# Four chained graph layers on one core: hand-written orders for the first three iterations, more load semaphores, and the 512-to-256 product summed in two halves

## The chip, the core and the metric

One Trainium2 chip, one of its cores, float32 inputs and outputs. The metric is the device time in microseconds (us) of one launch, from the first to the last instruction and what lies around them. TensorE is PE, VectorE is DVE, ScalarE is ACT, GpSimd is POOL, SyncE (which issues every transfer) is SP.

## What is computed

128 graphs of 128 nodes with 256 features, and an adjacency matrix per graph, pass four residual layers, each ended by a normalization over the features:

```python
x = _layernorm(x + _L0_gnn_ref(x, adj, W1, b1, gamma, beta, W2, b2), axis=-1)   # hypergraph convolutions 256->512->256
x = _layernorm(x + _L1_gnn_ref(x, adj, W), axis=-1)                             # x and its mean over neighbours, 512->256
x = _layernorm(x + _L2_gnn_ref(x, adj, W1, b1, W2, b2, W3, b3), axis=-1)        # three graph convolutions
x = _layernorm(x + _L3_gnn_ref(x, adj, kernel), axis=-1)                        # one more, masked where x is all zero
```

## The kernel before

Two graphs make a pair, and there are 64 pairs. The work on a pair is cut into stages, and a software pipeline runs them: in iteration n the first layer's stages work on pair n and n-1, the second's on n-2, the third's on n-3 and n-4, the fourth's on n-4 and n-5 (the table `LAG`). Iterations 0 to 7 and the last ones are unrolled, those between run in a hardware loop of four iterations a turn (`steps`, L175). Each engine runs one function `body(n, k)`, in which the order of its stages is written by hand; a stage that has no pair yet is skipped. Engines are tied by semaphores alone, and each engine's instructions run in the written order, so a wait holds everything behind it on that engine.

Products in high precision are split: a float32 matrix is rounded to `_hi`, the rest is `_lo`, and `product` (L257) issues three matmuls for each block: hi by hi, hi by lo, lo by hi. ACT makes most `_hi`, DVE or POOL the `_lo`.

The stages on PE that the prediction speaks of, for a pair p: `G` (operands BH, HT), its transpose `Tr` (ident, Gd), `Gx` (GT, x_in), `R` (24 matmuls of 256 columns, w1T by gx, the 256-to-512 product), `P` (L367: 24 matmuls of 258 columns, r by w2c, the 512-to-256 product, and two of one column, sq by ones, for the mean square), `GP` (p_f, GT), `xT` (ident, x), `XAB` (x1T by wab), `AXB` (xbw by A), `Ax2` (A_f, x), then `H1` and the others of the later layers. PSUM has eight banks of 512 columns; `BANK` gives each stage its own, and P uses two, one per graph.

P before: for each graph 12 matmuls over all four blocks of r and then its one-column matmul. It waits at its start for `r_hi[1]`, `r_lo` and `sq_sum`:

```python
pe.wait_ge(r_hi[1], upto(p))
pe.wait_ge(r_lo, upto(p))
pe.wait_ge(sq_sum, upto(p))
```

POOL makes r_lo in two halves (L978, L980) with one semaphore after the second, then adds the squares (L983, L985), then A_lo.

In the first iterations there is also the work on the weights, which are loaded into buffers that later hold data: w1T is split into hi (ACT, L466) and lo (POOL, L957); w2 is scaled (`scale_w2`, L686 and L688), its column means come from four matmuls with ones (w2g, ones), it is centred and split (`centre_w2`, L694 to L708), and beta by w2 is four matmuls (n_s, beta_b); wab, the three v and wk are split as well, the last four on POOL in iteration 1. DVE's edge counts of a pair (`prep`: L791 HT to L825 be_parts) and the scaling of G (L786, L795, L801, L811 Gd) are mixed in one sequence. DVE begins with constants and then waits for three small loads that share the semaphore `small_loaded`.

## Time and profile before

| | us |
|---|---|
| median of 3 runs | 1478.44 (1476.14 to 1479.6) |
| the profiled execution | 1476.8 |
| its span, first to last instruction | 1475.0 |
| PE busy | 1419.1 (96%) |
| DVE busy | 1152.0 (78%) |
| ACT busy | 1050.5 (71%) |
| POOL busy | 887.7 (60%) |

Matmuls are pipelined and overlap, so PE's busy time is time in which at least one is under way. The clock column of the windows gives the share of TensorE's full clock that was granted. A timeline merges equal instructions that follow each other: start, length, engine, line, operation, and in brackets the engine's idle time before it and what ended it.

### The profile page before, as it was taken

Reading aid. Unit: us, or ns where it says so; the run is one execution under the profiler, and the core shown is the slowest. Engines: PE = TensorE matmul, PEld = TensorE weight load, DVE = VectorE, ACT = ScalarE, POOL = GpSimd, SP = SyncE. Lnnn points to the kernel's source line nnn. Section 1 sums busy time; section 2 is a strip of 40 time slices with the busy share of each in tenths; the row PEclk is TensorE's granted clock in tenths of the full one; section 3 lists DMA queues with packets and bytes.
Section 4 is the critical chain, followed back from the end, with each engine's and each line's share of the span. In section 5 each row is a group of like instructions: output and inputs, shape, how many; then the busy total and the mean of one; then the engine's idle time right before and its main releaser. Section 6 shows DMA issues by size and latency. Waiting matters only on the chain. (4 is left out here: it accounts for less than half of the span.)

```text
span 1475.0 us, 34371 instructions
## 1 busy us (share of the span) xinstructions
PE 1419.1 (96%) x10896; PEld 1352.9 (92%) x10896; DVE 1152.0 (78%) x4063; ACT 1050.5 (71%) x2377; POOL 887.7 (60%) x841
## 2 busy tenths in 40 slices
PE   4899999999999999999999999999999999999974
PEld 4799999999999999999999999999999999999974
DVE  5678887887887878878878878788788788787763
ACT  3477777777777777777777777777777777767753
POOL 4455765665665665675675576566566566566542
PEclk9999999999999999999999999999999999999997
DMA  3001011011001001101101101101101100110000
GB/s 123 22 23 37 19 38 36 18 36 36 23 31 36 25 29 36 35 19 36 36 18 36 36 18 36 36 18 36 36 18 36 36 25 28 36 33 12 16 15 22
DMA packets 29419, 45.45 MB, mean 31 GB/s; under 512 B 3392, under 2 KB 11712, under 8 KB 29376
## 3 DMA queue, kind: packets, MB, share of 16 engines
q1 hardware_dynamic: 29376, 44.91, 9.5%
q8 instruction: 22, 0.36, 0.1%
q14 instruction: 21, 0.17, 0.0%
HBM read 28.12 MB, written 16.78 MB: 30 GB/s over the span
## 5 line engine op out<-in xcount | busy, mean ns | idle before, releaser
L957 POOL TENSOR_TENSOR h_lo<-h_f,h_hi 128x512 fp32r<-128x512 f32 x128 | 164.6, 1286 | 338.9 <-ACT h_hi L466 338.9
L714 DVE BATCH_NORM_STATS2 n_st<-n_s 128x6 f32<-128x256 f32 x512 | 188.6, 411 | 7.5 <-POOL n_s L990 5.2
L481 ACT ACTIVATE n_std<-n_mv,eps_c 128x2 f32<-128x2 f32 x256 | 74.7, 292 | 166.7 <-DVE n_mv L719 166.5
L972 POOL TENSOR_TENSOR n_s<-tk,mask 128x512 f32<-128x512 f32 x64 | 66.6, 1040 | 168.6 <-issue 82.8
L255 PE MATMUL psum<-w2c_hi,r_hi 128*128 128x258 f32 x512 | 150.4, 294 | 6.4 <-POOL sq L985 4.7
L255 PE MATMUL psum<-v_hi,h_hi 128*128 128x256 f32 x512 | 149.8, 292 | 5.0 <-issue 5.0
L494 ACT ACTIVATE h_f<-psum,columns 128x256 f32<-128x256 f32 x256 | 107.5, 471 | 54.4 <-PE psum L255 54.4
L255 PE MATMUL psum<-w2c_lo,r_hi 128*128 128x258 f32 x512 | 145.5, 284 | 0.0
L255 PE MATMUL psum<-v_lo,h_hi 128*128 128x256 f32 x512 | 145.4, 284 | 0.0
L255 PE MATMUL psum<-v_hi,h_lo 128*128 128x256 f32 x512 | 145.1, 283 | 0.0
L255 PE MATMUL psum<-gx_hi,w1T_hi 128*128 128x256 f32 x512 | 143.3, 280 | 1.3 <-DVE gx_lo L663 1.3
L255 PE MATMUL psum<-w2c_hi,r_lo 128*128 128x258 f32 x512 | 144.4, 282 | 0.0
L255 PE MATMUL psum<-gx_hi,w1T_lo 128*128 128x256 f32 x512 | 142.9, 279 | 0.0
L255 PE MATMUL psum<-gx_lo,w1T_hi 128*128 128x256 f32 x512 | 142.9, 279 | 0.0
L255 PE MATMUL psum<-A_f,x 128*128 128x128 f32 x1024 | 137.3, 278 | 4.8 <-ACT x L588 3.9
L255 PEld LDWEIGHTS psum<-A_f,x 128*128 128x128 f32 x1024 | 127.0, 194 | 5.2 <-ACT x L588 4.2
L978 POOL TENSOR_TENSOR r_lo<-r_f,r_hi 128x512 fp32r<-128x512 f32 x64 | 83.2, 1301 | 58.4 <-ACT r_hi L466 58.3
L255 PE MATMUL psum<-wab_hi,x1T_hi 128*128 128x512 f32 x256 | 106.8, 417 | 1.5 <-ACT x1T_hi L466 1.5
L663 DVE TENSOR_TENSOR ax_lo<-psum,ax_hi 128x512 fp32r<-128x512 f32 x128 | 87.9, 687 | 25.8 <-ACT ax_hi L466 25.8
L588 ACT ACTIVATE x<-n_s,n_shift,n_rstd 128x256 f32<-128x256 f32 x128 | 70.1, 595 | 48.6 <-DVE n_shift L731 48.6
L255 PEld LDWEIGHTS psum<-w2c_hi,r_hi 128*128 128x128 f32 x512 | 97.6, 191 | 7.1 <-issue 7.1
L255 PEld LDWEIGHTS psum<-v_hi,h_hi 128*128 128x128 f32 x512 | 97.8, 191 | 5.5 <-issue 5.5
(154 smaller groups left out, 5344.2 us busy)
## 6 DMA issues: line engine op xcount, KB each, us to landing
x_in<-x_in_dram SPq DMA_DIRECT2D x64, 256.0 KB, 2.6
out<-x SPq DMA_DIRECT2D x64, 256.0 KB, 2.0
at_in<-adjT SPq DMA_DIRECT2D x64, 128.0 KB, 2.1
r_f<-w1T_in SPq DMA_DIRECT2D x1, 512.0 KB, 5.4
n_s<-w2T_in SPq DMA_DIRECT2D x2, 256.0 KB, 5.7
h_f<-wab_in SPq DMA_DIRECT2D x2, 256.0 KB, 6.1
rows<-rows_in SPq DMA_DIRECT2D x1, 256.0 KB, 4.5
xa<-v_in SPq DMA_DIRECT2D x1, 256.0 KB, 6.0
```

Source lines behind the costliest of these rows:

```text
L255: return pe.matmul(o, a, b, start=start, stop=stop)
L481: act.activation(nm.std[:], nm.mv[:, :, 1], ACT.Sqrt, bias=eps_c[:, 0:1]).then_inc(nm.rooted, 1)
L494: return act.activation(dst[:, m].rearrange("p g c -> p (g c)"), psum[:, BANK[stage] + extra, (m % 2) * 2 * C:(m % 2 + 1) * 2 * C], ACT.Re ...
L588: last = act.activation(x3[:, g, :], n3.s[:, g, :], ACT.Identity, scale=n3.rstd[:, g:g + 1], bias=n3.shift[:, g:g + 1])
L663: return dve.tensor_tensor(dst[1][:], src, f(dst[0][:]), ALU.subtract).then_inc(signal, 1)
L714: last = dve.bn_stats(nm.st[:, g, :], nm.s[:, g, :])
L957: return pool.tensor_tensor(dst[1][:], src, f(dst[0][:]), ALU.subtract).then_inc(signal, 1)
L972: pool.tensor_tensor(n4.s[:], tk[:], bc(mask[:], [C, 2, D], 2), ALU.mult).then_inc(tk_masked, 1)
L978: pool.tensor_tensor(r_s[1][:, 0:2], r_f[:, 0:2], f(r_s[0][:, 0:2]), ALU.subtract)
```

## The change

The first three iterations (n = 0, 1, 2; `FILL = 3`) no longer come from `body` but from a function `fill` on each engine with its own order. The stages have become small functions that both `fill` and `body` call; for n of 3 and more the written order is as before. In the fill three stages use other banks (`bank`). The loads have more semaphores and another order, w1T is loaded and split in two halves, and its lo part is made on DVE instead of POOL. The three v and wk are loaded into buffers that are free until later (x3, x4, tk), so their splits can stand at the end of the fill. `P` sums the first two blocks of r for both graphs and then the other two, and `r_lo` has a semaphore for each half. Cut to its core:

```diff
+        def bank(stage, pair):
+            filling = isinstance(pair, int)
+            if filling and stage == "Tr" and pair in (1, 2):
+                return 3
+            if filling and stage == "GP" and pair == 0:
+                return 2
+            if filling and stage == "xT" and pair == 0:
+                return 6
+            return BANK[stage]
...
-            load(0, 0)
-            sp.dma_start(ident[:], eye).then_inc(small_loaded, 16)
-            sp.dma_start(columns_s[:], columns).then_inc(small_loaded, 16)
-            sp.dma_start(rows_b[:], rows.partition_broadcast(C)).then_inc(small_loaded, 16)
...
+            def fill():
+                sp.dma_start(at_in[:, 0], adjT[0]).then_inc(at_loaded[0], 16)
+                sp.dma_start(ident[:], eye).then_inc(eye_loaded, 16)
+                sp.dma_start(columns_s[:], columns).then_inc(columns_loaded, 16)
+                sp.dma_start(x_in[:, 0], x[0]).then_inc(x_loaded[0], 16)
+                for h in range(2):
+                    sp.dma_start(w2T_f[h], w2T[:, 2 * h:2 * h + 2]).then_inc(w2_loaded, 16)
+                for h in range(2):
+                    half = slice(h * 2 * C, (h + 1) * 2 * C)
+                    sp.dma_start(w1T_f[:, :, half], w1T[:, :, half]).then_inc(w1_loaded[h], 16)
+                load(1)
+                sp.dma_start(rows_b[:], rows.partition_broadcast(C)).then_inc(rows_loaded, 16)
+                for kk in range(KD):
+                    sp.dma_start(wab_f[kk], wab[:, kk]).then_inc(wab_loaded, 16)
+                load(2)
+                for dst, src in ((v_f[0], v1), (v_f[1], v2), (v_f[2], v3), (wk_f, wk)):
+                    sp.dma_start(dst, src).then_inc(v_loaded, 16)
+                load(3)
+                input_free(0)
+                load(4)
 
             def body(n, k):
-                if first(n, 0):
...
+            def P(n, k):
+                p = n - 1
+                if first(n, 1):
+                    pe.wait_ge(w2c_lo, 1)
+                if begun(n - 2):
+                    if not first(n, 2):
+                        pe.wait_ge(x1T_lo, upto(n - 2))
+                    pe.wait_ge(p_made, upto(n - 2))
+                for h in range(2):
+                    pe.wait_ge(r_lo[h], upto(p))
+                    for g in range(2):
+                        product(psum[:, BANK["P"] + g, 0:D + 2],
+                                [(part(r_s, ALL, m, g), part(w2c_s, ALL, m)) for m in (2 * h, 2 * h + 1)],
+                                start=h == 0, stop=h == 1)
+                pe.wait_ge(sq_sum, upto(p))
+                for g in range(2):
+                    last = mm(psum[:, BANK["P"] + g, D + 2:D + 3], sq1[:, g, :], ones[:, 0:1], True, True)
+                last.then_inc(pe_did["P"], 1)
...
+            def fill():
+                G(0, 0)
+                Tr(0, 0)
+                Gx(0, 0)
+                w2_columns()
+                R(1, 1)
+                G(1, 1)
+                Tr(1, 1)
+                Gx(1, 1)
+                P(1, 1)
+                betaW_rows()
+                R(2, 2)
+                GP(1, 1)
+                G(2, 2)
+                P(2, 2)
+                xT(2, 2)
+                Tr(2, 2)
+                Gx(2, 2)
+                XAB(2, 2)
+                GP(2, 2)
+                AXB(2, 2)
             def body(n, k):
                 if active("R", n):
...
+            def fill():
+                act.wait_ge(consts_step, 1)
+                act.activation(h_std[:, 0:1], eps_c[:], ACT.Sqrt).then_inc(table_loaded, 1)
+                act.wait_ge(table_loaded, 1)
+                act.wait_ge(columns_loaded, 16)
+                copy_GT(0, 0)
+                split_w1(0)
+                split_gx(0, 0)
+                split_w1(1)
+                relu_r(1, 1, 0)
+                round_r(1, 1, 0)
+                relu_r(1, 1, 1)
+                round_r(1, 1, 1)
+                square_r(1, 1)
+                copy_GT(1, 1)
+                split_gx(1, 1)
+                copy_A(1, 1)
+                act.wait_ge(wab_loaded, 16 * KD)
+                for kk in range(KD):
+                    copy(wab_s[0][:, kk], wab_f[kk]).then_inc(wab_hi, 1)
+                square_mean(1, 1)
+                root_h(1, 1)
+                relu_r(2, 2, 0)
+                round_r(2, 2, 0)
+                relu_r(2, 2, 1)
+                round_r(2, 2, 1)
+                root(n1, 0)
+                square_r(2, 2)
+                copy_A(2, 2)
+                split_x1T(2, 2)
+                square_mean(2, 2)
+                copy_GT(2, 2)
+                root_h(2, 2)
+                split_gx(2, 2)
+                act.wait_ge(v_loaded, 16 * 4)
+                for dst, src in ((v_s[0], v_f[0]), (v_s[1], v_f[1])):
+                    copy(dst[0][:], src).then_inc(v_hi, 1)
+                out_XAB(2, 2)
+                for dst, src in ((v_s[2], v_f[2]), (wk_s, wk_f)):
+                    copy(dst[0][:], src).then_inc(v_hi, 1)
+                root(n1, 1)
+                root(n2, 0)
             def body(n, k):
...
+                prep(-1, -1)
+                scale_G(0, 0)
+                dve.wait_ge(columns_loaded, 16)
+                dve.wait_ge(w2_loaded, 16 * 2)
+                for m in range(KH):
+                    dve.tensor_scalar(w2g[:, m, :], w2T_f[m // 2][:, m % 2], gamma_c[:, m:m + 1], None,
+                                      ALU.mult).then_inc(w2_scaled, 1)
+                split_w1(0)
+                split_gx(0, 0)
+                split_w1(1)
+                dve.wait_ge(w2_sums, 1)
+                dve.tensor_scalar(w2mean[:], psum[:, 2, 0:D], 1.0 / DH, None, ALU.mult).then_inc(w2_mean, 1)
+                prep(0, 0)
+                dve.wait_ge(w2_mean, 1)
+                dve.wait_ge(w2_scaled, KH)
+                dve.tensor_tensor(w2g[:], w2g[:], bc(w2mean[:], [C, KH, D], 1), ALU.subtract).then_inc(w2_centred, 1)
+                dve.wait_ge(w2_centred, 1)
+                dve.tensor_copy(w2c_s[0][:, :, 0:D], w2g[:]).then_inc(w2c_hi, 1)
+                scale_G(1, 1)
+                dve.wait_ge(w2c_hi, 1)
+                dve.tensor_tensor(w2c_s[1][:, :, 0:D], w2g[:], f(w2c_s[0][:, :, 0:D]),
+                                  ALU.subtract).then_inc(w2c_lo, 1)
+                split_gx(1, 1)
+                for m in range(KH):
+                    dve.tensor_scalar(beta_b[:, m, :], ones[:], beta_c[:, m:m + 1], None,
+                                      ALU.mult).then_inc(beta_made, 1)
+                dve.wait_ge(rows_loaded, 16)
+                dve.tensor_scalar(b2half[:], rows_b[:, 0], 0.5, None, ALU.mult).then_inc(consts_made, 1)
+                prep(1, 1)
+                dve.wait_ge(betaW_sums, 1)
+                dve.tensor_copy(betaW[:], psum[:, 3, 0:D]).then_inc(betaW_made, 1)
+                wide_var(1, 1)
+                wide_invert(1, 1)
+                make_p(1, 1)
+                dve.wait_ge(wab_hi, KD)
+                for kk in range(KD):
+                    dve.tensor_tensor(wab_s[1][:, kk], wab_f[kk], f(wab_s[0][:, kk]),
+                                      ALU.subtract).then_inc(wab_lo, 1)
+                sum_n1(1, 1)
+                stats_alone(n1, 0)
+                make_x1(2, 2)
+                scale_G(2, 2)
+                split_x1T(2, 2)
+                wide_var(2, 2)
+                wide_invert(2, 2)
+                make_p(2, 2)
+                split_gx(2, 2)
+                prep(2, 2)
+                split_xbw(2, 2)
+                sum_n1(2, 2)
+                stats_alone(n1, 1)
+                node_degree_max(2, 2)
+                node_degree_recip(2, 2)
+                make_agg(2, 2)
+                sum_n2(2, 2)
+                stats_alone(n2, 0)
+                invert(n2, 0)
+                shift(n2, 0)
...
+            def low_r(n, k, h):
+                p = n - 1
+                pool.wait_ge(r_hi[h], upto(p))
+                if begun(p - 1):
+                    pool.wait_ge(pe_did["P"], upto(p - 1))
+                half = slice(2 * h, 2 * h + 2)
+                pool.tensor_tensor(r_s[1][:, half], r_f[:, half], f(r_s[0][:, half]),
+                                   ALU.subtract).then_inc(r_lo[h], 1)
...
+            def fill():
+                make_BH(-1, -1)
+                make_BH(0, 0)
+                low_r(1, 1, 0)
+                low_r(1, 1, 1)
+                add_squares(1, 1)
+                low_A(1, 1)
+                make_BH(1, 1)
+                make_xb(1, 1)
+                low_r(2, 2, 0)
+                low_r(2, 2, 1)
+                add_squares(2, 2)
+                low_A(2, 2)
+                make_xb(2, 2)
+                make_BH(2, 2)
+                pool.wait_ge(v_hi, 4)
+                for dst, src in ((v_s[0], v_f[0]), (v_s[1], v_f[1]), (v_s[2], v_f[2]), (wk_s, wk_f)):
+                    lo(dst, src, v_lo)
 
             def body(n, k):
-                if first(n, 0):
-                    pool.wait_ge(w1_loaded, 16)
-                    pool.wait_ge(w1_hi, 1)
```

Where the instructions now stand. TensorE, from the end of the first R to the second R; gx and w1T are R's operands, n_s and beta_b those of beta by w2, w2c and r those of P. Before:

```order
L255 MATMUL psum<-gx_hi,w1T_lo 128x256
L255 MATMUL psum<-n_s,beta_b 128x256 x4
L255 MATMUL psum<-BH,HT 128x130 x4
L255 MATMUL psum<-w2c_hi,r_hi 128x258
...
L255 MATMUL psum<-ones,sq 128x1
...
L255 MATMUL psum<-ones,sq 128x1
L402 MATMUL psum<-ident,Gd 128x128 x2
L255 MATMUL psum<-GT,x_in 128x128 x4
L255 MATMUL psum<-p_f,GT 128x256 x2
L255 MATMUL psum<-gx_hi,w1T_hi 128x256
```

Now:

```order
L279 MATMUL psum<-gx_hi,w1T_lo 128x256
L279 MATMUL psum<-BH,HT 128x130 x4
L329 MATMUL psum<-ident,Gd 128x128 x2
L279 MATMUL psum<-GT,x_in 128x128 x4
L279 MATMUL psum<-w2c_hi,r_hi 128x258
...
L279 MATMUL psum<-w2c_hi,r_lo 128x258
L279 MATMUL psum<-ones,sq 128x1 x2
L279 MATMUL psum<-n_s,beta_b 128x256 x4
L279 MATMUL psum<-gx_hi,w1T_hi 128x256
...
L279 MATMUL psum<-p_f,GT 128x256 x2
```

Tr and Gx of pair 1 have moved ahead of P of pair 0, beta by w2 behind it, and R of pair 1 ahead of GP; the rows left out repeat the three operand pairs of the product.

VectorE, from its constants to the first split of gx. Before:

```order
L678 TENSOR_SCALAR w2c_lo<-ones 128x4 x2
L680 TENSOR_SCALAR b2half<-rows 128x256
L791 TENSOR_SCALAR HT<-at_in 128x256
L798 TENSOR_REDUCE ht_count<-HT 128x2
...
L825 TENSOR_TENSOR be_parts<-be_parts,be_r 128x2
L786 TENSOR_SCALAR dn_max<-psum 128x2
L791 TENSOR_SCALAR HT<-at_in 128x256
L795 RECIPROCAL dn_inv<-dn_max 128x2
L798 TENSOR_REDUCE ht_count<-HT 128x2
L801 SCALAR_TENSOR_TENSOR dinv<-psum,dn_inv 128x2
...
L811 TENSOR_TENSOR Gd<-psum,dinv 128x256
```

Now:

```order
L1024 TENSOR_SCALAR w2c_lo<-ones 128x4 x2
L903 TENSOR_SCALAR HT<-at_in 128x256
L907 TENSOR_REDUCE ht_count<-HT 128x2
...
L928 TENSOR_TENSOR be_parts<-be_parts,be_r 128x2
L881 TENSOR_SCALAR dn_max<-psum 128x2
L885 RECIPROCAL dn_inv<-dn_max 128x2
L889 SCALAR_TENSOR_TENSOR dinv<-psum,dn_inv 128x2
L896 TENSOR_TENSOR Gd<-psum,dinv 128x256
L1031 TENSOR_SCALAR w2g<-n_s,columns 128x256 x4
L1008 TENSOR_TENSOR w1T_lo<-r_f,w1T_hi 128x2x256
L817 TENSOR_TENSOR gx_lo<-psum,gx_hi 128x512
```

The edge counts of pair 0 (HT to be_parts) no longer stand behind b2half, the scaling of G of pair 0 (dn_max to Gd) no longer has the edge counts of pair 1 mixed into it, and half of w1T's lo part has come from POOL.

ScalarE, from the relu of pair 1 (r_f) to A, in iteration 2. Before:

```order
L481 ACTIVATE n_std<-n_mv,eps_c 128x2
L494 ACTIVATE r_f<-psum,columns 128x256 x4
L466 ACTIVATE x1T_hi<-psum 128x512
L466 ACTIVATE r_hi<-r_f 128x512 x2
L547 ACTIVATE sq<-r_f 128x1024
L466 ACTIVATE A_hi<-at_in 128x256
L466 ACTIVATE A_f<-at_in 128x256
```

Now:

```order
L591 ACTIVATE r_f<-psum,columns 128x256 x2
L567 ACTIVATE r_hi<-r_f 128x512
L591 ACTIVATE r_f<-psum,columns 128x256 x2
L567 ACTIVATE r_hi<-r_f 128x512
L581 ACTIVATE n_std<-n_mv,eps_c 128x2
L622 ACTIVATE sq<-r_f 128x1024
L567 ACTIVATE A_hi<-at_in 128x256
L567 ACTIVATE A_f<-at_in 128x256
L567 ACTIVATE x1T_hi<-psum 128x512
```

The square of r (sq) now stands behind n_std of pair 0, and x1T_hi behind A.

## Rows read from the trace of the kernel before

**Rows 1.** Windows: us, then PE, PEld, DVE, ACT, POOL busy, clock, DMA share, GB/s.

```profile
0.00:62.26 62.26, 37.03 (x225) 32.69 (x225) 36.26 (x120) 22.78 (x50) 25.57 (x29) 0.97 0.26 86
...
96.20:1388.40 1292.20, 1290.69 (x10032) 1234.76 (x10031) 1047.05 (x3710) 959.27 (x2181) 809.90 (x765) 1.00 0.09 29
...
1388.40:1475.00 86.60, 58.49 (x399) 54.47 (x397) 44.10 (x161) 46.21 (x98) 30.55 (x26) 0.86 0.05 19
```

**Rows 2.** Timeline of PE in the fill: start, us, engine, line, operation [idle before].

```profile
10.37 1.12 PE L255 MATMUL psum<-BH,HT 128*128 128x130 f32 x4 [10.37 <-POOL BH L1001]
...
13.91 0.66 PE L402 MATMUL psum<-ident,Gd 128*128 128x128 f32 x2 [2.42 <-DVE Gd L811]
...
15.05 2.08 PE L255 MATMUL psum<-GT,x_in 128*128 128x128 f32 x8 [0.47 <-ACT GT L466]
...
20.12 0.47 PE L255 MATMUL psum<-gx_hi,w1T_hi 128*128 128x256 f32 x1
...
23.06 1.89 PE L255 MATMUL psum<-n_s,beta_b 128*128 128x256 f32 x8
...
30.06 0.36 PE L255 MATMUL psum<-w2c_hi,r_hi 128*128 128x258 f32 x1 [4.72 <-POOL sq L985]
...
38.77 0.47 PE L255 MATMUL psum<-gx_hi,w1T_hi 128*128 128x256 f32 x1
```

**Rows 3.** Windows, the same columns: the start of P of pair 0.

```profile
30.00:34.00 4.00, 3.94 (x20) 3.97 (x21) 0.00 (x0) 0.00 (x0) 4.00 (x5) 0.57 0.00 0
```

**Rows 4.** Timeline of DVE in the fill.

```profile
7.16 0.29 DVE L680 TENSOR_SCALAR b2half<-rows 128x256 f32<-128x256 f32 x1 [5.30 <-DMA rows<-rows_in]
...
7.37 0.29 DVE L791 TENSOR_SCALAR HT<-at_in 128x256 fp32r<-128x256 f32 x1
...
8.83 0.15 DVE L825 TENSOR_TENSOR be_parts<-be_parts,be_r 128x2 f32<-128x2 f32 x1
...
11.62 1.16 DVE L791 TENSOR_SCALAR HT<-at_in 128x256 fp32r<-128x256 f32 x1
...
13.35 0.42 DVE L811 TENSOR_TENSOR Gd<-psum,dinv 128x256 f32<-128x256 f32 x1
...
39.88 0.75 DVE L714 BATCH_NORM_STATS2 n_st<-n_s 128x6 f32<-128x256 f32 x2
...
48.90 0.68 DVE L847 TENSOR_TENSOR xbw_lo<-psum,xbw_hi 128x512 fp32r<-128x512 f32 x1
```

**Rows 5.** The tile at_in up to 40 us: how long its five loads took.

```profile
DMA to landing us min/median/max: 2.1/6.0/6.9
```

**Rows 6.** Timeline of POOL in the fill.

```profile
9.14 1.18 POOL L1001 TENSOR_TENSOR BH<-HT,be_parts 128x256 fp32r<-128x256 f32 x2 [8.68 <-DVE be_parts L825]
...
27.75 1.27 POOL L983 TENSOR_TENSOR sq<-sq 128x512 f32<-128x512 f32 x1
...
29.09 0.72 POOL L985 TENSOR_TENSOR sq<-sq 128x256 f32<-128x256 f32 x1
```

**Rows 7.** Timeline of ACT, iterations 2 and 3.

```profile
44.60 1.05 ACT L547 ACTIVATE sq<-r_f 128x1024 f32<-128x1024 f32 x1
...
59.59 1.07 ACT L514 ACTIVATE x<-n_s,n_shift,n_rstd 128x256 f32<-128x256 f32 x2
...
60.57 1.54 ACT L494 ACTIVATE r_f<-psum,columns 128x256 f32<-128x256 f32 x4
```

**Rows 8.** Timeline of PE in the loop: between the graphs of P.

```profile
703.27 0.28 PE L255 MATMUL psum<-ones,sq 128*128 128x1 f32 x2
703.41 0.37 PE L255 MATMUL psum<-w2c_hi,r_hi 128*128 128x258 f32 x1
703.62 0.28 PE L255 MATMUL psum<-w2c_lo,r_hi 128*128 128x258 f32 x1
```

**Rows 9.** Waits of the weight loads, 140 to 1400 us: total, times, longest.

```profile
PEld psum L255 <- DVE p_f L895: 9.7, 45, 0.3
```

**Rows 10.** Timeline of ACT in the loop.

```profile
706.87 0.15 ACT L597 ACTIVATE h_mean<-psum 128x2 f32<-128x2 f32 x1
```

More of the change, by code:

```diff
@@ L27 @@
 BANKS = 8
+FILL = 3
 UNROLL = 4
@@ new lines, in betaW_rows @@
+            def betaW_rows():
+                pe.wait_ge(beta_made, KH)
+                for m in range(KH):
+                    last = mm(psum[:, 3, 0:D], beta_b[:, m, :], w2T_f[m // 2][:, m % 2], m == 0, m == KH - 1)
+                last.then_inc(betaW_sums, 1)
+            def fill():
[19 more added lines that the diff above has]
+                AXB(2, 2)
```

953 lines of the change are left out of this document (499 added, 454 removed).

## The prediction

> **What bounds it now.** I read the windows first, then the timeline of each engine in the fill, then the loop. They cut the span at 62.26 us, the start of the first Ax2, where the full pipeline begins, and where the drain begins. Between, PE is busy 1290.69 of 1292.20 us; before the first Ax2 it is busy 37.03 of 62.26, after the loop 58.49 of 86.60 [rows 1]. So of PE's idle time 25.2 us lie in the fill, 1.5 in the middle and 28.1 in the drain. The change rewrites the fill and leaves the drain's order. Since the middle has no slack on PE, an Ax2 that comes earlier ought to move the end by as much.
>
> The timeline of PE in the fill shows where the 25.2 us are: 10.37 before the first G, released by POOL's BH; 2.42 before Tr, released by DVE's Gd; 4.72 before P of pair 0, released by POOL's sum of squares; the rest in pieces of 1.6 us or less [rows 2]. It shows a second loss too. P of pair 0 starts after that idle stretch, and from 30 to 34 us the granted clock is 0.57, so mostly the lower of the two levels, 1.2 GHz instead of 2.4 [rows 3].
>
> **The start.** DVE does nothing for 5.30 us but wait for the third of three loads under one semaphore, though the edge counts behind it need only at_in [rows 4]. Now they wait for that alone. It is still the first load, issued at 0.75, and the quickest at_in landed 2.1 us after its issue [rows 5], at 2.9. The counts take 1.6 (7.37 to the end at 8.98), POOL's BH 1.35 with its start delay (8.98 to 10.32) [rows 4, 6]. G starts at about 5.9: **4.5 us less idle**.
>
> G takes 1.12 us. The scaling of G took 2.24 us to the end of Gd at 13.77, as it was mixed with the next pair's counts, HT's 1.16 among them [rows 4]. Alone it is three small steps at 0.2 (as between the small steps before be_parts) and Gd's 0.42, so Tr waits 1.2, not 2.42: **1.2 less**. GT and Gx follow at their old distances. From Gx to R it was 5.07 us (15.05 to 20.12) [rows 2]; in it the work on w2 hides gx's split and now hides w1T's lo, whose two halves cost DVE 1.3 in place of one long one on POOL. R of pair 0 comes at 14.5 instead of 20.1.
>
> **From R to the second iteration.** Before, P waited 4.72 us for relu, rounding, r_lo and squares. Now G, Tr and Gx of pair 1 stand there, and P asks for the squares (1.27 and 0.72 on POOL [rows 6]) at its end only. The new order has its own waits. R ends at 17.4; w2mean, the counts (1.6) and BH (1.35) let G start at 17.9: 0.5. Tr waits for DVE: 1.1. Gx waits for the copy of GT: 0.5. P then finds r_lo made, and the lower clock should not come, as no idle stretch here is longer than 1.2 us where the one before P was 4.72. The window has 20 matmuls in 4.0 us; at the 0.12 of R (24 in 2.94 us) they take 2.4: **1.6 us of busy time less** [rows 2, 3].
>
> So Tr stands at 19.6, Gx at 20.6, P at 21.6. P is 26 matmuls, 3.1 us, beta by w2 1.5 (23.06 to the next work at 24.6), and R of pair 1 comes near 26.2, not 38.77 [rows 2]; with its 2.94, GP's 1.0 and G's half of 1.12 P of pair 1 starts near 30.7 and its product ends at 33.6, but its squares come late: on ACT the root of n1 now stands ahead of the square, and that root waits for GP, the sum, and the statistics (0.75 and 0.3) on DVE, until about 32.2; then 1.05 on ACT and 2.1 on POOL [rows 4, 6, 7]. PE waits **1.8**. Behind it stand xT, Tr, Gx and all that follows. Then 0.95 before Gx of pair 2 (x1T_hi and h_mean lie ahead of GT on ACT); 1.0 before AXB (xbw_hi and xa, each about half of sq's 1.05, and xbw_lo's 0.68 on DVE, less GP's length [rows 4, 7]).
>
> **Into iteration 3.** From AXB's end DVE has two small steps (0.4), agg and the sum of n2 (0.7 to 0.9 each, as xbw_lo), the statistics (1.05), then with ACT's root three small steps (0.9), and only then x1 for xT (0.75): 4.9 to 5.2 with the delays. R and G cover 3.5; with what n1's own statistics push DVE back, xT waits 1.9. ACT's x (1.07) and four relus (1.54) [rows 7] stand before Ax2: 1.3 more.
>
> **The sum of the fill.** Idle after: 5.9 + 1.2 + 0.5 + 0.5 + 1.1 + 0.5 + 1.8 + 0.95 + 1.0 + 1.9 + 1.3 = 16.65 us, against 25.2: 8.6 less. With the clock's 1.6 that is **10.2 us**, Ax2 at 52 instead of 62.26. Two prices the trace doesn't show. When the clock rises: before, the matmuls ran slow until about 20.1, after 5 us of nearly unbroken work; now such work begins at 9.4. If it rises as late against that, R runs at full rate; if R runs at the lower level throughout, it takes 24 x 0.1 = 2.4 us more. I take 0.3, for the full case is the nearest row. And POOL's four splits of v and wk (512 columns and some 1.3 each, as the first sum of squares [rows 6]), which lay under P, now lie over DVE's chain into iteration 3. HT took 0.29 us with POOL idle, but 1.16 where POOL worked [rows 4]; the price is from nothing to twice that 0.87. I take 0.5. The fill gives 10.2 - 0.8 = 9.4, with bounds 7 to 11.
>
> The Trainium skill (SBUF — State Buffer, "Who interferes with whom") says that a VectorE operation with two SBUF inputs and a GpSimd operation that reads SBUF exclude each other for the whole instruction. By it the sum and x1 of that chain could each wait out a full split, 2.6 us in all by the row above.
>
> **P in two halves, in the loop.** Nothing waits there for r_lo. But the one-column matmuls are now together at the end. Before, the first stood between the graphs: it starts at 703.27, graph 1's first product at 703.41, its second at 703.62, so 0.21 us for a step that elsewhere takes 0.12 [rows 8]. Over 64 pairs the 0.085 saved would be 5.4 us. I don't count on it. In 45 of the 58 iterations between 140 and 1400 us the weight load of GP waited for p_f [rows 9]. p_f hangs on h_mean. ACT began it at 706.87 with no idle time before it [rows 10], while P's last matmul, twelve steps of 0.12 behind 703.41, had started at 704.9. So ACT's own queue sets that moment, not P, and what P saves the wait for p_f takes. At the 13 others up to 0.085 each may stay: 0 to 5.4 us, I take **0.6**, near the lower end, for most iterations wait.
>
> The drain keeps its order; its stretches at the lower clock may fall otherwise, 1 us either way, taken as nothing.
>
> **Sum.** 9.4 + 0.6 = 10.0 us off. The profiled execution took 1476.8, which is 1.6 below the median of the runs shown, well within their spread. From it the result is 1466.8; against the median of 1478.44 it is **1468.4 us**, which I forecast, 0.7% faster. About 0.2%, 3 us, is what a measurement of this kernel tells from no change.
>
> **Rivals.**
>
> *Half of it* (0.15). The new waits are longer than reckoned: the square behind n1's root, the collision with POOL, w2 landing late, R at the lower clock. Each alone costs 1 to 2.5 us; two or three together leave 4 to 6: 1473.4. For it: every stage I moved is on a chain of four engines with little cover. Against: the first wait's 4.5 us depends on one load only.
>
> *The loop keeps P's saving* (0.12). If the ring gets shorter with P, 5.4 instead of 0.6: 1463.6. For it: in 13 iterations PE didn't wait. Against: the 45.
>
> *Alternating banks cost time* (0.03). Now P goes graph 0, 1, 0, 1, two more changes of bank a pair, 128 in all, and leaves an accumulation open in each. The middle has no slack, so it pays all of it: from 10.0/128 = 0.08 us a change the gain is gone. If a change had to let the matmul before it end, 0.28 instead of 0.12 [rows 8], it costs 0.16, 20.5 us in all: 1488.9, slower. Against: PE is busy without a break through the middle although XAB changes banks as well [rows 1].
>
> The Trainium skill (TensorE: Matmul & The Clock Gate, "A second HAM failure mode: psum-queue depth-cycling") warns of just that: a kernel that cycled through PSUM banks kept falling to the lower clock between its matmul groups. With P at 1.2 GHz in every iteration 24 x 0.1 x 64 would be 150 us more. The clock column reads 1.00 through the loop [rows 1], and by the rule it should not.
>
> *It does not do what it says* (0.03). Something in the middle sets the end by itself, or what starts early waits in iterations 3 to 7: 1478. Against: PE's 1.5 us of idle in the middle.
>
> The forecast has 0.67. Faster by over 0.2% holds it, the half and the loop's saving, 0.94; within 0.2% 0.03; slower 0.03. The range takes the bounds of the fill and of the loop (11 + 5.4 off: 1462.0) and reaches over the half: 1462.0 to 1474.0.
>
> **What would show it.** PE's first G at 5.9, not 10.4; R of pair 0 at 14.5; no clock below full between 14.5 and the drain; the wait for sq before P's last matmuls in iteration 2, near 1.8; the first Ax2 at 52 to 53; the loop's period as it was, with more wait for p_f. Wrong if Ax2 is early and the end is not, or if the iterations' period changed by more than 0.1 us.

## The result, and the profile after

The changed kernel took **1472.1 us**, the median of 6 runs (1469.8 to 1472.7). Before took 1478.1 us beside it, in 6 runs. The ratio is 0.9957, with a 95% interval from 0.9944 to 0.9969: 6.0 us faster, where 10.0 was forecast. The profiled execution took 1472.7 us with a span of 1470.8, that is 4.1 and 4.2 us less than the profiled one of before. So the traces show 4.2 of the 6.0 us.

| | before | after |
|---|---|---|
| median, us | 1478.1 | 1472.1 |
| span of the profiled run | 1475.0 | 1470.8 |
| first G | 10.37 | 5.86 |
| R of pair 0 | 20.12 | 14.32 |
| R of pair 1 | 38.77 | 29.57 |
| first Ax2 | 62.26 | 56.10 |
| GP of iteration 3 | 74.7 | 69.4 |
| last GP | 1410.0 | 1405.0 |
| from there to the end | 65.0 | 65.8 |

So in the profiled executions the fill gave 6.2 us up to the first Ax2 and 5.3 up to GP of iteration 3, the loop kept all but 0.3 of that, and the drain lost 0.8.

The timeline of PE in the fill answers to [rows 2]. These are its waits, each with its releaser, and two of the operations that ran slowly:

```profile
5.86 1.12 PE L279 MATMUL psum<-BH,HT 128*128 128x130 f32 x4 [5.86 <-POOL BH L1233]
8.17 0.66 PE L329 MATMUL psum<-ident,Gd 128*128 128x128 f32 x2 [1.20 <-DVE Gd L896]
9.39 2.08 PE L279 MATMUL psum<-GT,x_in 128*128 128x128 f32 x8 [0.56 <-ACT GT L567]
...
19.55 0.66 PE L279 MATMUL psum<-BH,HT 128*128 128x130 f32 x4 [1.70 <-POOL BH L1233]
...
21.31 0.44 PE L329 MATMUL psum<-ident,Gd 128*128 128x128 f32 x2 [1.10 <-DVE Gd L896]
22.22 2.08 PE L279 MATMUL psum<-GT,x_in 128*128 128x128 f32 x8 [0.47 <-ACT GT L567]
...
27.95 1.97 PE L279 MATMUL psum<-n_s,beta_b 128*128 128x256 f32 x8
29.57 0.47 PE L279 MATMUL psum<-gx_hi,w1T_hi 128*128 128x256 f32 x1
...
34.90 0.36 PE L279 MATMUL psum<-w2c_hi,r_hi 128*128 128x258 f32 x1 [0.89 <-POOL r_lo L1213]
...
54.36 0.66 PE L394 MATMUL psum<-ident,x 128*128 128x128 f32 x4 [3.26 <-DVE x L857]
56.10 1.95 PE L279 MATMUL psum<-A_f,x 128*128 128x128 f32 x8 [1.08 <-ACT r_f L591]
```

The first three waits are as forecast (5.9, 1.2, 0.5). The fourth, before G of pair 1, is 1.70 where 0.5 was forecast, and xT of iteration 3 waits 3.26, not 1.9. The same Gx takes 1.16 us at full clock (at 41.04) and 2.08 at 22.22; Ax2 took 1.13 before and takes 1.95.

The windows say why (us, then PE, PEld, DVE, ACT, POOL busy, clock, DMA share, GB/s). They answer to [rows 3]:

```profile
18.00:22.00 4.00, 1.10 (x6) 0.72 (x6) 2.64 (x7) 2.55 (x6) 4.00 (x5) 1.00 0.00 0
22.00:25.00 3.00, 2.78 (x13) 2.78 (x14) 1.06 (x2) 0.83 (x3) 2.89 (x2) 0.51 0.00 0
...
51.00:56.00 5.00, 0.76 (x5) 0.42 (x4) 2.73 (x11) 2.88 (x8) 1.71 (x2) 1.00 0.01 2
56.00:59.00 3.00, 2.90 (x11) 2.74 (x12) 0.97 (x2) 2.39 (x5) 1.96 (x2) 0.53 0.00 0
```

From 18 to 22 us PE was busy 1.10 of 4.00 us, six matmuls with no gap above 1.7 us around them; then the granted clock is the lower level, 1.2 GHz, for about 3 us of nearly unbroken work. From 51 to 56 it was busy 0.76 of 5.00, with one gap of 3.26 us, and the same follows. The slow stretch of before is gone, and two others have come. (The clock column can't be read at the very start: up to 14 us it says 1.00, though the first Gx takes 2.08 us, as it does later at 0.51.)

Two collisions of DVE and POOL stand behind the two long waits. POOL's timeline first, then DVE's:

```profile
16.95 2.55 POOL L1233 TENSOR_TENSOR BH<-HT,be_parts 128x256 fp32r<-128x256 f32 x2 [11.14 <-DVE be_parts L928]
```

```profile
16.78 1.22 DVE L1041 TENSOR_TENSOR w2g<-w2g,w2mean 128x1024 f32<-128x1024 f32 x1
...
49.84 1.74 DVE L993 SCALAR_TENSOR_TENSOR n_s<-agg,x 128x512 f32<-128x512 f32 x1
```

BH takes 1.18 when DVE leaves it alone [rows 6], and 2.55 beside the centring of w2 and the rounding behind it. The sum of n2 takes 0.68 in the loop and 1.74 here, beside POOL's splits of v.

In the loop, the waits of the weight loads (total, times, longest) answer to [rows 9], and GP of iterations 3 and later, first and last start, shows the loop's length, of before and of after:

```profile
PEld psum L279 <- DVE p_f L964: 11.1, 55, 0.3
```

```profile
L255 PE MATMUL psum<-p_f,GT x248: 379/379/483, 74.7 to 1410.0; 128*128 128x256 f32 x124
```

```profile
L279 PE MATMUL psum<-p_f,GT x248: 379/379/483, 69.4 to 1405.0; 128*128 128x256 f32 x124
```

That is 62 groups of four matmuls, so 61 intervals, and the 0.8 us from the first to the last matmul of the last group: together 1335.3 us before, 1335.6 after, 21.9 us an iteration in both. So P's saving in the loop is nothing. Below, "the 61 intervals" are counted in this same way.

### The profile page after: what moved, and what is told of

The parts are those of the page before. It is cut to its first block and busy times, and to the rows that moved or that the text cites. A ratio compares the mean times of both kernels' runs of the same rounds, so it can differ in the third digit from the quotient of the medians.

```text
span 1470.8 us, 34536 instructions
## 1 busy us (share of the span) xinstructions
PE 1420.3 (97%) x10896; PEld 1355.6 (92%) x10896; DVE 1151.5 (78%) x4066; ACT 1051.4 (71%) x2378; POOL 889.0 (60%) x840
## 5 line engine op out<-in xcount | busy, mean ns | idle before, releaser
L586 ACT ACTIVATE x<-n_s,n_shift,n_rstd 128x256 f32<-128x256 f32 x384 | 208.6, 591 | 65.9 <-DVE n_shift L847 63.1
L1213 POOL TENSOR_TENSOR r_lo<-r_f,r_hi 128x512 fp32r<-128x512 f32 x128 | 164.0, 1304 | 38.2 <-ACT r_hi L567 38.1
L279 PE MATMUL psum<-w2c_hi,r_hi 128*128 128x258 f32 x512 | 145.0, 283 | 0.9 <-POOL r_lo L1213 0.9
L591 ACT ACTIVATE r_f<-psum,columns 128x256 f32<-128x256 f32 x256 | 99.1, 463 | 4.1 <-PE psum L279 4.1
```

What stands on the lines that cost most here:

```text
L279: return pe.matmul(o, a, b, start=start, stop=stop)
L586: last = act.activation(dst[:, g, :], nm.s[:, g, :], ACT.Identity, scale=nm.rstd[:, g:g + 1], bias=nm.shift[:, g:g + 1])
L591: return act.activation(dst[:, m].rearrange("p g c -> p (g c)"), psum[:, BANK[stage] + extra, (m % 2) * 2 * C:(m % 2 + 1) * 2 * C], ACT.Re ...
L1213: pool.tensor_tensor(r_s[1][:, half], r_f[:, half], f(r_s[0][:, half]), ALU.subtract).then_inc(r_lo[h], 1)
```

## The experiments

The runs of before beside these had medians of 1477.7 us (b_start, b_p, a_old_p, a_veps), 1477.4 (b_order, a_prep, a_sq, a_v), 1477.1 (a_alt, a_warm, a_nov) and 1477.8 (a_best). Each ratio is to these. After was not run again beside them, only before: what is said "under after" or "above after" sets medians of different sets of runs side by side and is good to about 1 us.

### The start alone, in the kernel before

b_start moves two waits, and the step on b2half that hangs on one of them, and nothing else:

```diff
-            dve.wait_ge(small_loaded, 16 * 3)
-            dve.tensor_scalar(b2half[:], rows_b[:, 0], ...)
+                if first(n, 0):          # behind prep of pairs 0 and 1
+                    dve.wait_ge(small_loaded, 16 * 3)
+                    dve.tensor_scalar(b2half[:], rows_b[:, 0], ...)
                     scale_w2()
-            pool.wait_ge(consts_made, 1)  # from POOL's start to ahead of w1T's low part
```

> The kernel before, with one thing of the change: DVE's wait for the three small loads and POOL's wait for b2half move behind the edge counts of pairs 0 and 1. My theory: this alone gives the start's 4.5 us. First G at 5.9, R of pair 0 at 15.6 instead of 20.1, time 1478.1 - 4.5 = 1473.6. Rival: the loads of w1T and w2T, which keep their place behind the rows, bound R and the centring of w2; then R moves by 2 us or less and the time is 1476 or more.

1476.5 us, ratio 0.9993 (0.9984 to 1.0002): no difference that can be measured. Its timeline of PE has the early G, and behind it a new wait:

```profile
5.88 1.11 PE L255 MATMUL psum<-BH,HT 128*128 128x130 f32 x4 [5.88 <-POOL BH L999]
12.51 0.66 PE L402 MATMUL psum<-ident,Gd 128*128 128x128 f32 x2 [5.52 <-DVE Gd L808]
```

DVE's timeline names what stood in front:

```profile
11.08 0.29 DVE L788 TENSOR_SCALAR HT<-at_in 128x256 fp32r<-128x256 f32 x1 [3.89 <-DMA at_in<-adjT]
```

In DVE's queue of before, the counts of pair 1 are interleaved with the scaling of G of pair 0, and they wait for at_in of pair 1, which comes behind w1T and w2T. My theory fell, and so did the rival, which named R and w2. The semaphore only pays with the order.

b_order adds that order (scaling of G, scaling of w2, then the counts of pair 1):

```diff
+                if first(n, 0):
+                    ...  # degree_max, recip, inverse and Gd of pair 0
+                    dve.wait_ge(small_loaded, 16 * 3)
+                    ...
+                    scale_w2()
+                    ...  # HT, ht_count, be, be_parts of pair 1
+                else:
+                    ...  # interleaved as before
```

> The kernel before with its own wait for at_in as in b_start, and DVE's order of the first iteration changed too: the scaling of G of pair 0 and of w2 first, then the edge counts of pair 1. In b_start the first G came at 5.9 but Tr then waited 5.5 us, since in DVE's queue the counts of pair 1 stood between the steps of the scaling and waited for at_in of pair 1. My theory: it takes both, the semaphore and the order. Tr at 8.2, Gx at 9.4, R of pair 0 between 14.5 and 17 (w1T and w2T set it), and the time 2 to 4.5 us under before: 1473.2 to 1475.7. Rival: P of pair 0 hangs on the chain from w2's load through w2's centring, and nothing is gained: 1477.

1473.8 us, ratio 0.9979 (0.9970 to 0.9989). Tr came at 8.21, but R of pair 0 only at 17.8. DVE waited 2.25 us for w2T, which lies behind w1T in SP's queue, and then its first scaling of w2 took 2.44 us instead of the 0.34 of the next ones:

```profile
10.52 2.44 DVE L683 TENSOR_SCALAR w2g<-n_s,columns 128x256 f32<-128x256 f32 x1 [2.25 <-DMA n_s<-w2T_in]
```

Beside it POOL split w1T from 10.47 to 12.82, the work that the change gives to DVE. The gain is 3.6 us, inside the expectation. The profiled execution doesn't show it: it was the slowest of the 11 (1477.2), R of pair 0 came early, but the clock was at the lower level in parts of 25 to 40 us, and the first Ax2 stood at 63.27, behind the 62.26 of before. So the semaphore and DVE's order together are shown to pay; that the rest of the change's start comes from SP's order and from w1T's split on DVE is read off these waits and not tested alone.

### P in two halves

b_p is the kernel before with P, and the two semaphores of r_lo, as in the change's diff. a_old_p is the changed kernel with the old P from iteration 3 on, and a_alt changes graph with every matmul there:

```diff
 a_old_p
-                    for h in range(2):
-                        pe.wait_ge(r_lo[h], upto(p))
-                        for g in range(2):
-                            product(..., start=h == 0, stop=h == 1)
-                    pe.wait_ge(sq_sum, upto(p))
+                    for h in range(2):
+                        pe.wait_ge(r_lo[h], upto(p))
+                    pe.wait_ge(sq_sum, upto(p))
+                    for g in range(2):
+                        product(...)
+                        last = mm(psum[:, BANK["P"] + g, D + 2:D + 3], sq1[:, g, :], ones[:, 0:1], True, True)
 a_alt
-                    for h in range(2):
-                        for g in range(2):
-                            product(psum[:, BANK["P"] + g, 0:D + 2], [... for m in (2 * h, 2 * h + 1)])
+                    for m in range(KH):
+                        for x, y in ((0, 0), (0, 1), (1, 0)):
+                            for g in range(2):
+                                mm(psum[:, BANK["P"] + g, 0:D + 2], r_s[x][:, m, g], w2c_s[y][:, m], ...)
```

> The kernel before, with the two-half P alone, in the fill and the loop. My theory: in the fill P of pair 0 no longer waits for the two sums of squares, 1.27 + 0.72 us, and the loop keeps nothing: 1478.1 - 2.0 = 1476.1, with a period of 21.8 to 22.2 us per four... that is, per iteration group as before and more wait for p_f than 9.7 us. Rival, the loop keeps 0.085 us a pair: 1476.1 - 5.4 = 1470.7. Rival, alternating banks cost 0.16 us a change: above 1490.

1475.6 us, ratio 0.9984 (0.9975 to 0.9993): 2.1 us less, as expected. P of pair 0 waited 1.18 for r_lo, not 4.72 for the squares, and started at 28.06 instead of 30.06, though the first G came 1.2 us later. The 61 intervals took 1335.8 us. This profiled execution too was the slowest of its 11 (1478.3): from 40 to 47 us its clock was at the lower level, and what P had gained was gone at the first Ax2 (63.58).

> The changed kernel, but from iteration 3 on P goes graph by graph as before, each with its one-column matmul behind it. My theory: the loop's saving was all taken by the wait for p_f, so the time stays within 0.6 us of 1472.1 and the wait for p_f falls from 11.1 to about 9.7 us. Rival, the loop kept part of it: up to 1477.5. Rival, the changes of bank cost something: below 1471.

1473.3 us, ratio 0.9965 (0.9952 to 0.9979). GP of iteration 3 and the last one started at 69.4 and 1404.8, so the 61 intervals took 1335.4 us against 1335.6: the loop's length doesn't depend on the form of P. The median is 1.2 above after, outside the expected 0.6, but the two intervals overlap, and the trace has the same loop and the same start of GP. The expected size of the wait was wrong as well: it is 11.6 us, not 9.7. The listed total of that wait is no ledger for the time.

> The changed kernel, from iteration 3 on P changes graph, and so PSUM bank, with every matmul: 23 changes a pair in place of 3, with the same matmuls. My theory: a change of bank costs nothing; time within 0.7 of after, matmuls of P 0.12 us apart. Rival: a change costs 0.01 us or more: 20 x 61 x 0.01 = 12 us and above, 1484.

1474.5 us, ratio 0.9981 (0.9971 to 0.9990). That is 2.4 above after and outside the expected 0.7, but not in the loop. There the 61 intervals took 1335.6 us, as in after. The matmuls of P, now merged in pairs over the two graphs, begin 0.24 us apart, 0.12 each, and the clock of the window is full:

```profile
701.15 0.40 PE L279 MATMUL psum<-w2c_hi,r_hi 128*128 128x258 f32 x2
701.39 0.41 PE L279 MATMUL psum<-w2c_lo,r_hi 128*128 128x258 f32 x2
701.63 0.40 PE L279 MATMUL psum<-w2c_hi,r_lo 128*128 128x258 f32 x2
```

```profile
66.00:1385.00 1319.00, 1316.93 (x10233) 1261.73 (x10232) 1066.42 (x3759) 975.54 (x2217) 826.91 (x782) 1.00 0.09 29
```

A change of bank costs nothing here. The 4.5 us by which GP of iteration 3 comes later in its profiled run (73.9) lie in the fill, whose orders are those of after: Gx of pair 2, and XAB behind it, ran at the lower clock there, Gx in 2.08 us where after had 1.16. Which short stretches of the fill fall to the lower level differs between runs of one and the same order.

### Three reorderings in the fill

```diff
 a_prep (DVE)
+                prep(0, 0)
                 dve.wait_ge(w2_sums, 1)
                 dve.tensor_scalar(w2mean[:], psum[:, 2, 0:D], ...)
-                prep(0, 0)
 a_sq (ACT)
-                root(n1, 0)
                 square_r(2, 2)
+                root(n1, 0)
 a_v (ACT, then POOL)
                 square_mean(1, 1)
+                act.wait_ge(v_loaded, 16 * 4)
+                for dst, src in (...): copy(dst[0][:], src).then_inc(v_hi, 1)   # from around out_XAB(2, 2)
                 root_h(1, 1)
...
-                make_BH(2, 2)
                 pool.wait_ge(v_hi, 4)
                 for dst, src in (...): lo(dst, src, v_lo)
+                make_BH(2, 2)
```

> The changed kernel with DVE's edge counts of pair 1 ahead of w2mean, in the 1.5 us in which DVE waited for w2's sums. My theory: the missed 1.2 us before G of pair 1 come from POOL's BH (2.55 us beside DVE's centring of w2, 1.19 alone). BH starts at 15 and ends before R does; G of pair 1 waits 0 to 0.2 us instead of 1.7, Gx of pair 1 starts at 20.6, and if the clock does not fall before it, it takes 1.16 instead of 2.08 us. Time 1.5 to 3 us under after: 1469 to 1470.5. Rival: the collision only moves, since w2's centring now meets BH earlier or r_lo; P of pair 0 waits for w2c_lo instead, and the time stays within 0.7 of after.

> The changed kernel with ACT's square of pair 1 ahead of the root of n1. My theory: the wait before P's last matmuls in iteration 2 (0.90 us) goes, and xT of pair 0, already late, does not come later as DVE waits 0.3 us at most. First Ax2 0.8 us earlier, time 0.8 under after: 1471.3. Rival: Gx of pair 2 and xT wait longer by what was gained (x1 later): no change.

> The changed kernel with the splits of v and wk earlier: ACT's four high parts while it waits before root_h of pair 0, POOL's four low parts between xb and BH of iteration 2, where POOL was idle for 4.4 us and DVE's long operations read PSUM. My theory: the sum of n2 took 1.74 us beside POOL's splits; it takes 0.69 now, xT of iteration 3 waits 2.2 instead of 3.26 us, the first Ax2 comes 1.0 us earlier, and with less idle time the clock may hold, which gives 1 us more. Time 1 to 2.5 us under after: 1469.6 to 1471. Rival: BH of pair 3, now behind the splits, makes G late by what is gained, or the clock falls in any case: within 0.5 of after.

Their medians are 1470.6 (ratio 0.9942 to 0.9969), 1471.0 (0.9941 to 0.9968) and 1471.4 us (0.9945 to 0.9973), the second as expected, the first and third 0.1 and 0.4 above the ranges. The intervals overlap that of after, so the times alone don't prove a gain; the traces show each wait. In a_prep the wait before G of pair 1 is gone, and the first Ax2 comes at 54.05 instead of 56.10. BH still took 2.17 us beside the centring, but it began 2.0 us earlier. In a_sq the wait for the squares is 0.37 instead of 0.90, not gone, and the first Ax2 comes at 55.22. In a_v the sum of n2 took 0.69, and xT waits 2.20:

```profile
53.30 0.69 DVE L991 SCALAR_TENSOR_TENSOR n_s<-agg,x 128x512 f32<-128x512 f32 x1
```

```profile
56.78 0.66 PE L394 MATMUL psum<-ident,x 128*128 128x128 f32 x4 [2.20 <-DVE x L855]
```

In its profiled run that gain was lost (the first Ax2 at 58.51), as Gx of pair 2 and XAB behind it fell to the lower clock:

```profile
41.00:48.00 7.00, 6.30 (x19) 0.51 0.17 56
```

In this row the columns are us, PE busy, clock, DMA share and GB/s.

### The clock

a_warm puts matmuls whose results nobody uses ahead of PE's waits, 29 in the fill and 60 in the drain (not 64, as the expectation says):

```diff
+            WARM = {(1, 'G'): 5, (1, 'Tr'): 4, (1, 'Gx'): 1, (2, 'AXB'): 4, (3, 'xT'): 12, (3, 'Ax2'): 3,
+                    (65, 'xT'): 8, (65, 'AXB'): 8, ...}
+            def warm(n, stage):
+                for _ in range(WARM.get((n, stage), 0) if isinstance(n, int) else 0):
+                    mm(psum[:, 6 if n < 4 else 5, 0:2 * D], w1T_s[0][:, 0, 0:C], w1T_s[0][:, 0, 0:2 * D], True, True)
             def G(n, k):
+                warm(n, "G")
```

> The changed kernel with idle work for PE: matmuls of 512 columns into an unused bank stand ahead of waits, 5, 4 and 1 of them before G, Tr and Gx of pair 1, 4 before AXB of iteration 2, 12 and 3 before xT and Ax2 of iteration 3, and 64 in the drain before its longer waits, each group some 20% shorter than the wait. Nothing else changes, their results are not used. My theory: the clock fell to the lower level twice in the fill (22 to 25.5 and 56 to 59 us) because PE had been mostly idle in the 4 us before each, and that is the missing part of the forecast. With this work the clock stays at the upper level; the first P starts 0.9 us earlier, the first Ax2 takes 1.13 instead of 1.95 us and the fill gives 2.5 to 3.5 us; the drain, where 10 of 60 us run at the lower level, gives 1 to 3 us more. Time 3.5 to 6 us under after: 1466 to 1468.6. Rival: the clock falls on its own schedule whatever PE does, and the added matmuls delay the real ones: 1472 or more.

1463.7 us, ratio 0.9912 (0.9897 to 0.9927): **8.4 us under after** by the medians, 7.4 if each is taken against the before beside it, and more than expected. The clock stays up in both stretches. The windows of a_warm, with the columns of the first windows above:

```profile
18.00:22.00 4.00, 3.34 (x20) 2.52 (x21) 2.70 (x5) 1.27 (x2) 4.00 (x4) 1.00 0.00 0
22.00:25.00 3.00, 3.00 (x29) 3.00 (x27) 2.21 (x6) 2.25 (x5) 2.37 (x3) 1.00 0.03 8
...
51.00:56.00 5.00, 4.07 (x22) 3.08 (x22) 2.00 (x6) 5.00 (x11) 1.73 (x2) 1.00 0.00 2
56.00:59.00 3.00, 3.00 (x21) 2.70 (x20) 3.00 (x10) 1.84 (x5) 2.92 (x4) 1.00 0.00 0
```

The drain, of after and then of a_warm (us, PE busy, clock, DMA share, GB/s):

```profile
1400.00:1436.00 36.00, 27.35 (x184) 0.91 0.04 15
```

```profile
1400.00:1436.00 36.00, 32.50 (x217) 1.00 0.04 15
```

GP of iteration 3 came at 65.4 instead of 69.4, which is 4.0 us from the fill, the 61 intervals took 0.6 less, and from the last GP to the end it took 61.2 instead of 65.8 us, 4.6 from the drain. Of the 4.0 not all is the idle matmuls' work, for R of pair 0 already began 1.05 us earlier, and the first idle matmul stands behind it. R's first matmul in after, and then in a_warm:

```profile
14.32 0.78 PE L279 MATMUL psum<-gx_hi,w1T_hi 128*128 128x256 f32 x1
```

```profile
13.27 0.47 PE L279 MATMUL psum<-gx_hi,w1T_hi 128*128 128x256 f32 x1
```

Up to there both have the same order; what differs is when the matmuls on w2 pass from the slow pace to the fast one (in a_veps R began at 13.31, in a_nov at 13.48). That leaves about 3.0 us in the fill for the idle matmuls, an estimate from one execution of each. The Trainium skill (TensorE: Matmul & The Clock Gate, "The HAM clock gate") says that the gate follows how busy PE has been lately; the rows agree, with the clock at 0.51 behind 1.10 us of work in 4.00 and at 1.00 behind 3.34. The runs of a_warm lie within 1.2 us (4 runs), those of after within 2.9.

### What the wait for p_f costs

```diff
 a_veps
-                dve.scalar_tensor_tensor(out=h_veps[:], in0=h_var[:], scalar=LN_EPS,
-                                         in1=eps_c[:].to_broadcast([C, 2]), op0=ALU.add, op1=ALU.max)
+                dve.tensor_scalar(h_veps[:], h_var[:], LN_EPS, LN_EPS, ALU.add, ALU.max)
```

> The changed kernel, but the variance plus epsilon of the wide norm (h_veps) takes two constants instead of the constant and the tile eps_c: one SBUF input instead of two. In the loop it took 0.81 us beside POOL's work and 0.16 elsewhere, and it lies on the chain from P to p_f. My theory: p_f is 0.4 to 0.65 us earlier, PE's weight load no longer waits for it (11.1 us, 55 times), and the time falls by 6 to 11 us: 1461 to 1466. Rival 1: the wait for p_f covers the next one, for h1w or ax_hi or gx; the time falls by under 2 us. Rival 2: POOL's hold on DVE falls on the next two-input instruction instead, and p_f stays late: no change.

1474.4 us, ratio 0.9979 (0.9970 to 0.9987), not faster than after. The groups of DVE from 66 to 1380 us, of after and of a_veps (count, busy us, mean ns, idle before):

```profile
L948 DVE SCALAR_TENSOR_TENSOR h_veps<-h_var,eps_c 128x2 f32<-128x2 f32 x60 | 48.1, 802 | 2.1
```

```profile
L948 DVE TENSOR_SCALAR h_veps<-h_var 128x2 f32<-128x2 f32 x60 | 48.7, 811 | 2.1
```

The operation on 2 columns takes 0.8 us in either form. One of them in after:

```profile
702.21 0.81 DVE L948 SCALAR_TENSOR_TENSOR h_veps<-h_var,eps_c 128x2 f32<-128x2 f32 x1
```

It ends at 703.02, and POOL's xb, which ran from 701.70, ends at 703.00. In ten iterations across the loop, in after and in a_veps alike, the operation ended 0.02 to 0.03 us behind POOL's xb each time, and at 41.47 in the fill of after, where POOL is idle, it took 0.16. So the 0.8 us is what is left of POOL's instruction. My theory of the second input fell before it came to the question of p_f. The Trainium skill (SBUF — State Buffer, "Who interferes with whom") lists tensor_scalar among the operations that may enter a two-port mode and then exclude GpSimd. By that rule the one-input form waits as well; the row agrees, though no run here shows the mode itself.

a_nov therefore takes the step out instead; it leaves out the clamp of a variance below zero, and epsilon goes in as the bias of ACT's root:

```diff
                 dve.scalar_tensor_tensor(out=h_var[:], ..., op0=ALU.mult, op1=ALU.subtract).then_inc(hv, 1)
-                dve.wait_ge(hv, upto(n - 1))
-                dve.scalar_tensor_tensor(out=h_veps[:], in0=h_var[:], scalar=LN_EPS, ...).then_inc(hve, 1)
-                act.wait_ge(hve, upto(n - 1))
-                act.activation(h_std[:], h_veps[:], ACT.Sqrt).then_inc(hstd, 1)
+                act.wait_ge(hv, upto(n - 1))
+                act.activation(h_std[:], h_var[:], ACT.Sqrt, bias=eps_c[:, 0:1]).then_inc(hstd, 1)
```

> The changed kernel without the instruction that adds epsilon to the wide variance and clamps it (left out: the clamp of a variance below zero from rounding; epsilon goes in as the bias of ACT's root). With one SBUF input in place of two (a_veps) it still took 0.80 us, so that the number of inputs was not the cause. My theory: p_f comes 0.8 us earlier, and PE's weight load no longer waits for it (11.1 us, 55 times). If that wait is what PE pays for in the middle, the loop gets 0.1 to 0.2 us a pair shorter, 6 to 11 us: 1461 to 1466. Rival: the wait is hidden under PE's own pipeline or another wait takes its place at once (x1 of the next pair for xT): less than 2 us.

**1452.9 us**, ratio 0.9837 (0.9824 to 0.9851): 19.2 us under after, where I had expected 6 to 11. GP goes from 69.8 to 1385.2, so the 61 intervals took 1315.4 instead of 1335.6 us, 0.33 us less each:

```profile
L279 PE MATMUL psum<-p_f,GT x248: 379/379/483, 69.8 to 1385.2; 128*128 128x256 f32 x124
```

That is the wait in one iteration, read at PE's Gx and GP, first of after, then of a_nov:

```profile
703.22 1.06 PE L279 MATMUL psum<-GT,x_in 128*128 128x128 f32 x8
704.42 1.13 PE L279 MATMUL psum<-p_f,GT 128*128 128x256 f32 x4
```

```profile
694.12 1.06 PE L279 MATMUL psum<-GT,x_in 128*128 128x128 f32 x8
695.02 1.03 PE L279 MATMUL psum<-p_f,GT 128*128 128x256 f32 x4
```

From the start of Gx to that of GP it is 1.20 us in the one and 0.90 in the other. PE counts as busy in both, for the end of a pipelined matmul is modelled; the busy share of 1290.69 in 1292.20 us [rows 1] hid a wait of 0.3 us in every iteration, and the list of waits (11.1 us) showed about half of it.

### All of it together

a_best joins a_prep, a_sq, a_v, a_nov and a_warm, with 1 idle matmul instead of 5 before G of pair 1, 2 instead of 1 before Gx, and 8 instead of 12 before xT of iteration 3.

> Everything that helped, together, on the changed kernel: the counts of pair 1 ahead of w2mean (a_prep), the square of pair 1 ahead of n1's root (a_sq), the early splits of v and wk (a_v), the wide variance without its separate epsilon step (a_nov, the clamp below zero left out), and the idle matmuls of a_warm with the groups before G of pair 1 and xT of iteration 3 cut to 1 and 8, since those waits are shorter. If the savings add up: 1452.9 - 8.4 (a_warm against after) - 2.1 (a_prep's first Ax2) - 0.9 (a_sq's) - 1.0 (the sum of n2 in a_v) = 1440.5. Rival: with the clock held, the three reorderings hide behind one another, since they shorten the same waits: 1443 to 1445. A second rival: the shorter loop of a_nov meets another wait in the ring and gives back part: above 1446.

**1441.3 us** in 5 runs from 1441.3 to 1441.6, ratio 0.9754 (0.9741 to 0.9768): 36.5 us under before, 30.8 under after. The sum of the parts, 1440.5, was 0.8 off. The first Ax2:

```profile
50.87 1.13 PE L279 MATMUL psum<-A_f,x 128*128 128x128 f32 x8 [0.38 <-ACT r_f L609]
```

That is earlier than the 52 of the forecast. The fill could give what I had summed up, but only with the clock held and the collisions moved.

## Why the prediction was right, and where it was short

The direction and the range were right, the size was not: 6.0 us instead of 10.0. Of the rivals, "Half of it" (1473.4) lies nearer to the result than the forecast, and it named the causes: the collision with POOL and R or its neighbours at the lower clock.

**The start (4.5 us): right**, 5.86 against 5.9. My reason was half of it. I put it on the load's wait alone, and b_start shows no gain from that alone that can be measured; it needs DVE's new order, which I had priced at 1.2 us for Tr only.

**Tr and Gx (1.2, 0.5), R at 14.5: right**: 1.20, 0.56 and 14.32.

**"R ends at 17.4 [...] G start at 17.9: 0.5": wrong by 1.2.** BH was costed alone, at 1.35 with its start delay, and it took 2.55. I had not looked at what DVE does while POOL makes BH. The counts stood behind w2mean, where DVE was idle 1.50 us, and then w2's centring met BH.

**"the lower clock should not come, as no idle stretch here is longer than 1.2 us": the step that failed.** I read the length of the longest gap. What stood ahead of the first slow stretch was a sum of short ones, the longest 1.70, with 1.10 us of work in 4.00; ahead of the second it was 0.76 in 5.00, with a gap of 3.26 where I had forecast 1.9. The clock's 1.6 us that I counted as a gain was not gained: Gx took 2.08 us instead of 1.16, and P's matmuls ran 0.21 us apart instead of 0.12 up to 25.4, and the work on beta came at 27.95, so that R of pair 1 was at 29.57, not 26.2. Of these 3.4 us about 1.65 are G's lateness (19.55 against 17.9), most of the rest is the clock. From the first Ax2 to GP of iteration 3 it took 0.9 more than before. a_warm prices the clock at about 3.0 us in the fill, where the forecast was off by 4.0 in all. The two long waits add 1.2 and 1.4 us to that, and the 0.8 us of unknown prices that I had taken off are in both; so the shares of clock and collisions are not exact, as one brings on the other.

**The squares (1.8): right in sum, by luck.** 0.89 was paid before P of pair 1 for r_lo, a wait that I had not seen, and 0.90 at its end for the squares, half of what I had forecast. Gx of pair 2 waited 0.81 (0.95), AXB 1.15 (1.0), Ax2 1.08 (1.3).

**xT of iteration 3 (1.9): 3.26.** I allowed 0.5 for POOL's splits over DVE's chain. One of them held the sum of n2 for 1.05 us more. I had named the Trainium skill's rule (SBUF — State Buffer, "Who interferes with whom") with 2.6 us in all, and the trace bore it out for the sum, not for x1, whose 0.73 us (from 53.57) fell after the splits (to 52.71).

**P in halves in the loop (0.6): right**, it was 0. a_old_p shows it. Alternating banks: a_alt shows no cost with 23 changes a pair in place of 3, and the Trainium skill's warning of clock loss from cycling through banks (TensorE: Matmul & The Clock Gate, "A second HAM failure mode: psum-queue depth-cycling") is not borne out in this kernel, at a clock of 1.00.

**The drain (0): it cost 0.8** in the profiled run, inside the 1 us either way that I had named. The cause stays open: from the last GP on the mean clock was 0.83 in after and 0.81 in before, so it isn't simply more time at the lower level.

**Not seen at all:** "the middle has no slack". It had 20 us, the largest piece found here, in the wait which I used as evidence that P's saving would vanish.

## What to carry to other kernels

Cost a reordered start-up by engine pairs, not by engines: for each long VectorE operation ask what GpSimd runs beside it, and for each semaphore made finer, what now stands first in the queue behind it. Where TensorE works in short bursts between waits, allow for the lower clock in the stretch that follows, and try idle matmuls in the waits: here they also went with steadier runs. A single profiled execution can lie at the edge of its runs, so look where its time stands among them before reading a gain from it. When a wait repeats in every iteration of a loop whose engine seems 100% busy, measure start to start, and take a step out of the chain that feeds it before polishing anything outside the loop.

## What the runs showed of the hardware

- Gaps of 0.5 to 1.7 us, with 1.10 us of work in 4.00, stood ahead of a fall of the granted clock from 2.4 to 1.2 GHz that lasted about 3 us; the same stretch with 3.34 us of work kept it. Low stretches fell elsewhere in runs with the same order of the fill (after and a_alt). That this is why the runs of after spread over 2.9 us is not shown, but those of a_best, with the clock held, spread over 0.3.
- A VectorE operation on 2 columns takes 0.8 us on average beside GpSimd's work, with one SBUF input as with two, and 0.16 without it; in ten iterations each of after and a_veps it ended 0.02 to 0.03 us behind the GpSimd instruction beside it. One of 256 columns with one tensor input took 2.44 us instead of 0.34 beside a GpSimd instruction of 2.35.
- At the start of a run the clock column reads 1.00 while the first Gx takes 2.08 us, as at 0.51 later.
- 23 changes of PSUM bank in a product of 24 matmuls cost nothing measurable: 1335.6 us for 61 iterations with 3 or with 23.
- A wait of 0.33 us an iteration on the weight load of a matmul didn't show in TensorE's busy share, and removing its cause gave 20 us.
